# Self-attention and a frequency-split convolution: x loaded first in a turn, the scan and the low convolution later, the next image's scale and its value projection moved into the turn

## The chip, the cores and the metric

One core of one Trainium2 chip runs the whole program in one launch. The metric is device time in microseconds (us), lower is better. TensorE (PE) does the matmuls, ScalarE (ACT) exponentials and copies, VectorE (DVE) subtractions, maxima and sums, GpSimd (POOL) elementwise work and one reduction over partitions, SyncE (SP) issues all DMAs in one queue.

## The reference

x has 4 images of 256 channels and 64x64 pixels. Layer 0 is self-attention over the 4096 pixels of an image:

```
q = Wq x; k = Wk x; v = Wv x                    (32, 32 and 256 rows)
attn = softmax(q^T k / sqrt(32));  out = Wo (v attn^T);  x1 = gamma * out + x
```

Layer 1 works on each 8x8 patch of x1: `low` is the mean of 2x2 pixels, `high = p - up2(low)`; low goes through a 256x256 product, high and its copy rolled by one row go through a 256x512 product, each with a bias, a batch norm and a PReLU, and the output is `up2(low) + high`.

## The kernel before, in words

An image is cut into 8 chunks of 512 pixels, so there are 32 turns, one per chunk of queries. The values are not v but u = (Wo Wv) x, scaled by a number found from the largest |x| of the image so that they fit a pair of fp16 tensors (`uh`, `ul`). All probabilities are fp16 pairs too, so a product is three matmuls. While turn g weighs the values of its own image, it also projects one chunk of the next image (plan FULL, 24 turns); the turns of the last image have no projection (plan LAST, 7 turns), and the last turn is FINAL.

A turn has 32 steps t in a fixed order, `UNITS`. Sixteen steps are key tiles "d" (scores S by L593, two exponentials on ACT, L761 and L764, the low half on DVE, L1046, then twelve matmuls, L634 to L636), and sixteen are slots "k". A slot's probabilities come from the scores that the turn before saved (`saved`), take two exponentials (L772, L773) and a subtraction on DVE (L1051), go through a DMA transpose (L373) into `pt`, and are weighed by twelve matmuls (L647 to L649). A slot is subtracted three or four steps ahead of its use, so that the transpose has time. The order is d0 to d5, then k0, d6, k1, d7 and so on, and the last six steps are k10 to k15.

In between a plan gives each step small tasks of PE that use the PSUM banks M0 and M1 in turn. A task that takes a bank waits until the one before it on that bank was read:

- `kq` and `u 0`, `u 1`: the next image's keys and queries, and its values in two halves (L485). ACT reads a value half with the image's scale (L784), DVE makes the low half (L1078).
- `max j m`: 32 score blocks of the next turn's queries, whose maxima DVE takes (L946, and L950 with saving). `DOUBLE` lists the steps that hold two.
- `negmax`: the maxima of the 512 queries transposed (L528), for the next turn's `qcur`, which `finish_q` builds on DVE (L964 and L965). The first scores of the next turn wait for it.
- `y 0`, `y 1`: the attention output transposed, plus x (L1058). `low` and `high`: the two products of layer 1 on it (L485), read by ACT (L791, L797).

The scale of the image after next's values comes from a scan: in turn c of an image DVE takes the maximum |x| of chunk c (L903) at step `SCAN`, from `xr`, after which the same buffer is loaded with the residual. At the start of an image `before_image` runs `find_scale`: DVE reduces the 8 maxima (L908), POOL reduces over partitions (L1188, L1189), DVE finishes in four small steps (L910 to L918). ACT waits for the result before the first turn of the image. This happens three times inside the loop (ahead of turns 0, 8 and 16) and once in the start.

SP's queue is in program order and holds, per turn, 16 transposes, the q, u, x and out transfers, and in the last turn of an image the reload of all u tiles. `turn_slot(g, k)` is one transpose with its waits; what stands between two `turn_slot` calls is issued between two transposes.

Of the kernel before, what the change touches and what calls it, by code (L numbers as in the profile page):

```python
# [26 lines left out]
B, C, HW = 4, 256, 64 * 64  # L27
# [6 lines left out]
ALL = B * NCH  # L34
# [10 lines left out]
ROUND_X, ROUND_CONV, SCAN, NEGATIVE = 9, 14, 12, 26  # L45

DOUBLE = (8, 10, 15, 17, 25)
# [38 lines left out]
def steps_with_maxima(steps, first=3, doubled=DOUBLE):  # L86

    left = list(MAXIMA)
    t = first
    while left:  # L90
        for _ in range(2 if t in doubled else 1):
            j, m = left.pop(0)
            assert m not in TURNED or t > LOW_AT[slot_of(j, m)]
            steps.setdefault(t, []).append(("max", j, m))
        t += 1
    steps[t] = [("negmax",)]
    return steps
# [3 lines left out]
FULL = Plan(steps_with_maxima({0: [("kq",), ("u", 0)], 2: [("u", 1)], 5: [("y", 0)], 6: [("y", 1)], 19: [("low", 0)],  # L101
                               20: [("low", 1)], 21: [("high", 0)], 23: [("high", 1)]}))

LAST = Plan(steps_with_maxima({4: [("y", 0)], 5: [("y", 1)], 19: [("low", 0, 1)], 21: [("high", 0)], 23: [("high", 1)]},
                              doubled=(8, 10, 12, 15, 17, 26)),
# [9 lines left out]
def attention_conv(nc, x, wqk, wv, wo, phase_w, mag_w, params, gamma, alpha, out, q_dram):  # L115
# [7 lines left out]
    with ctx:  # L123
# [133 lines left out]
        def turns(eng, turn, before_image=None, before_last=None, image_end=None):  # L257


            inner = NCH - 1 if image_end else NCH  # L260
            with eng.Fori(0, B // 2 - 1) as pair_i:
                for parity in range(2):
                    if before_image:
                        before_image(pair_i * 2 + parity, parity)
                    with eng.Fori(0, inner) as c:
                        turn(pair_i * (2 * NCH) + parity * NCH + c, parity, c, FULL, scans=True)
                    if image_end:
                        image_end(pair_i * (2 * NCH) + parity * NCH + inner, parity, inner, scans=True)

            if before_image:  # L270
                before_image(B - 2, 0)
            with eng.Fori(0, inner) as c:
                turn((B - 2) * NCH + c, 0, c, FULL, scans=False)
            if image_end:
                image_end((B - 2) * NCH + inner, 0, inner, scans=False)
            if before_last:
                before_last()
            with eng.Fori(0, NCH - 1) as c:
                turn((B - 1) * NCH + c, 1, c, LAST, scans=False)
            turn(ALL - 1, 1, NCH - 1, FINAL, scans=False)  # L280
# [46 lines left out]
        def _(sp):  # L327
# [63 lines left out]
            def turn(g, parity, c, plan, scans, ends_image=False):  # L391
                slot = c if isinstance(c, int) else ds(c, 1)
                flat = (lambda dram: dram[slot]) if isinstance(c, int) else (lambda dram: dram[slot].rearrange("k q n -> (k q) n"))
                if plan is FULL:

                    sp.wait_ge(qsave_ready, NCH + g + 1)
                    sp.dma_start(flat(q_dram), qsave[96:128, :]).then_inc(qsave_free, 16)
# [8 lines left out]
                if plan is FULL:  # L406
                    emptied(sp, plan, g, ("u", 1))
                    sp.dma_start(flat(uh_dram), uh_next_flat[:, :]).then_inc(u_stored, 16)
                    sp.dma_start(flat(ul_dram), ul_next_flat[:, :]).then_inc(u_stored, 16)
# [4 lines left out]
                if plan is FULL:  # L414

                    sp.wait_ge(x_split[0], EVEN_FIRST + g)
                    gk = (g + 1 + NCH) % ALL
                    sp.dma_start(xb[:, :, :], x_v[ds(gk // NCH, 1), ds(gk % NCH, 1)]).then_inc(xb_loaded, 16)
                if ends_image:
                    sp.wait_ge(u_stored, 32 * g + 64)  # L420
                    sp.sem_inc(turn_seen, 1)
                    load_direct_u(g, 0)
# [8 lines left out]
                turn_slot(g, 4)  # L431
                if ends_image:
                    load_direct_u(g, 1)
                turn_slot(g, 5)
                turn_slot(g, 6)
# [3 lines left out]
                if scans:  # L439
                    sp.wait_ge(xs_scanned, g + 2)  # L440
                    sp.dma_start(xr[:, :, :], x_v[ds(g // NCH, 1), ds(g % NCH, 1)]).then_inc(xr_loaded, 16)
# [7 lines left out]
                turn_slot(g, 11)  # L449
                turn_slot(g, 12)  # L450
# [5 lines left out]
                if ends_image:  # L456
                    load_turned_u(g, TURNED[2])
                    load_turned_u(g, TURNED[3])
# [239 lines left out]
        def _(act):  # L698
# [76 lines left out]
            def take(bank, task, g, parity, c):  # L775

                kind = task[0]
                if kind == "kq":
                    nc.scalar.activation(kst[0:96, ds(c * CH + (1 - parity) * HW, CH)], bank[0:96, :], ACT.Copy).then_inc(k_hi, 1)
                    act.wait_ge(qsave_free, 16 * (NCH + g + 1))  # L780
                    nc.scalar.activation(qsave[96:128, :], bank[96:128, :], ACT.Copy).then_inc(qsave_ready, 1)
                elif kind == "u":
                    act.wait_ge(u_stored, 32 * g + 32)
                    nc.scalar.activation(uh_next[:, 2 * task[1]:2 * task[1] + 2, 0:C],  # L784
                                         bank[:, :].rearrange("p (m n) -> p m n", n=C),
                                         ACT.Copy, scale=uscale[1 - parity][:, 0:1]).then_inc(u_hi, 1)
# [57 lines left out]
            def before_image(image, parity):  # L844
                act.wait_ge(scaled, image + 2)

            turns(act, turn, before_image)
# [13 lines left out]
        def _(dve):  # L861
# [43 lines left out]

            def find_scale(image, parity):

                nc.vector.tensor_reduce(bnd[:, 0:1], amax[:, parity, :], AX.X, ALU.max).then_inc(bound, 1)  # L908
# [15 lines left out]
            dve.wait_ge(scanned0, NCH)  # L924
            find_scale(0, 0)
# [34 lines left out]

            def finish_q(bank, count, free):

                dve.wait_ge(nhi_ready, count)
                nc.vector.tensor_copy(qcur[0:96, :], qst[0:96, :].bitcast(f32))  # L964
# [58 lines left out]
            nc.vector.tensor_copy(nhi[96:128, :], M[n % 2][96:128, :]).then_inc(nhi_ready, 1)  # L1023
            finish_q(M[n % 2], 1, m_free[n % 2])
# [7 lines left out]
            def normalise(g):  # L1032
# [4 lines left out]
                gain = ogain[:, B - 1:B] if isinstance(g, int) else ogain[:, ds((g + (ALL - 1)) % ALL // NCH, 1)]  # L1037
# [59 lines left out]
            def finish_chunk(g):  # L1097

                dve.wait_ge(s_filled, ND * g + ND)
                finish_q(M[1], g + 2, m_free[1])  # L1100

            def turn(g, parity, c, plan, scans):
# [6 lines left out]
                for t in range(MT):  # L1109
# [6 lines left out]
                    if t == 1 and plan is not FINAL:  # L1116
                        low_q(g + 2)
                    if t == SCAN and scans:
# [7 lines left out]
                    if t == NEGATIVE:  # L1126
                        negative_parts(plan, g)
                if plan is FULL:
                    finish_chunk(g)

            def before_image(image, parity):

                dve.wait_ge(xs_scanned, image * NCH + 1)
                find_scale(image + 1, 1 - parity)

            turns(dve, turn, before_image)
# [127 lines left out]
```

## Time and profile before

| | us |
|---|---|
| median of 3 runs (lowest, highest) | 2344.87 (2343.41, 2346.97) |
| the profiled execution | 2340.0 |
| its span | 2337.9 |
| PE busy in the span | 2211.3 (95%) |
| DVE busy | 1753.7 (75%) |
| ACT busy | 1436.5 (61%) |
| POOL busy | 679.7 (29%) |
| mean granted clock of TensorE, as a share of full | 0.985 |

The span is the profiled execution without what lies around it (2.1 us). A busy PE in this view is not PE at its peak, since matmuls are drawn with their whole pipeline and overlap one another. What tells more is from which instruction to which the time runs, and what ended an idle stretch.

### The profile page before, as it was taken

The numbers are of one execution on the slowest core, as the hardware profiler recorded it, in microseconds if no ns is written. First come the engines' busy times: TensorE is split into PE (matmuls) and PEld (weight loads), VectorE is DVE, ScalarE is ACT, GpSimd is POOL, SyncE is SP. The second block draws the span as 40 slices with busy tenths as digits, with TensorE's granted clock in tenths as the row PEclk, the third lists the DMA queues.
The fourth block names the chain that finished last, engine by engine and source line by source line (L and its number), as shares of the span: only waits on it lengthen the run. The fifth ranks groups of instructions, "written<-read, shape, count | busy, mean of one in ns | idle before, by whom it ended". The sixth has DMA issues, their size and how long they took to land.

```text
span 2337.9 us, 48151 instructions
## 1 busy us (share of the span) xinstructions
PE 2211.3 (95%) x16373; PEld 1763.5 (75%) x16373; DVE 1753.7 (75%) x3388; ACT 1436.5 (61%) x2547; POOL 679.7 (29%) x891
## 2 busy tenths in 40 slices
PE   5799999999989999999998999999999999999997
PEld 4577777777767777777776877777777777777776
DVE  6777787777767777877776777777877777778764
ACT  3456666656656666666665666576666656666664
POOL 3232332232322323322332222323322232233221
PEclk8799999999999999999999999999999999999998
DMA  5154444355553554443474433544445444344443
GB/s 167 44 113 112 99 103 109 71 112 113 133 131 72 109 116 99 105 105 81 100 169 103 101 83 75 111 98 95 103 106 131 83 93 88 76 84 89 84 86 67
DMA packets 596617, 235.02 MB, mean 101 GB/s; under 512 B 547072, under 2 KB 548352, under 8 KB 596576
## 3 DMA queue, kind: packets, MB, share of 16 engines
q1 hardware_dynamic: 596576, 234.51, 45.7%
q8 instruction: 22, 0.36, 0.1%
q14 instruction: 19, 0.16, 0.0%
HBM read 67.67 MB, written 32.53 MB: 43 GB/s over the span
## 4 chain that ended last, share of the span: by engine, by line
PE 69%; DVE 11%; issue 8%; DMA 5%; ACT 4%; SPq 1%; POOL 1%; DVEq 0%; ACTq 0%; POOLq 0%
PE M L485 13%; PE M L522 8%; PE O L647 7%; PE O L634 7%; PE O L649 7%; PE O L636 7%; PE O L648 7%; PE O L635 7%; PE S L593 4%; DVE pq L1051 3%; DMA xr<-in_x 2%; DVE pmax L946 2%; DMA pt<-pq 2%; DVE saved L950 2%; DVE pl L1046 1%
## 5 line engine op out<-in xcount | busy, mean ns | idle before, releaser
L761 ACT ACTIVATE ph<-S 128x512 f16<-128x512 f32 x512 | 307.1, 600 | 480.5 <-PE S L593 479.4
L647 PE MATMUL O<-uh,pt 128*128 128x257 f16 x2048 | 568.5, 278 | 9.6 <-DMA pt<-pq 9.1
L950 DVE TENSOR_SCALAR_CACHE_REDUCE saved<-M 128x512 f32<-128x512 f32 x512 | 346.1, 687 | 305.8 <-PE M L522 303.5
L634 PE MATMUL O<-uh,ph 128*128 128x257 f16 x2048 | 570.4, 278 | 4.2 <-DVE pl L1046 3.8
L636 PE MATMUL O<-uh,pl 128*128 128x257 f16 x2048 | 563.2, 275 | 0.0
L635 PE MATMUL O<-ul,ph 128*128 128x256 f16 x2048 | 561.9, 274 | 0.0
L649 PE MATMUL O<-uh,pt 128*128 128x257 f16 x2048 | 558.9, 273 | 0.0
L648 PE MATMUL O<-ul,pt 128*128 128x256 f16 x2048 | 555.7, 271 | 0.0
L522 PE MATMUL M<-kst,qst 96*128 (+1 forms) x1024 | 435.7, 447 | 25.6 <-DVE pmax L946 13.3
L1046 DVE TENSOR_TENSOR pl<-p,ph 128x512 f16<-128x512 f32 x512 | 396.4, 775 | 53.8 <-ACT p L764 52.4
L772 ACT ACTIVATE pq<-saved,nbias 128x512 f16<-128x512 f32 x512 | 369.2, 721 | 47.3 <-DMA pt<-pq 47.3
L1051 DVE TENSOR_TENSOR pq<-saved,pq 128x512 f16<-128x512 f32 x512 | 383.8, 750 | 19.2 <-ACT saved L773 19.0
L946 DVE TENSOR_REDUCE pmax<-M 128x1 f32<-128x512 f32 (+1 forms) x512 | 339.9, 683 | 40.1 <-PE M L522 38.1
L773 ACT ACTIVATE saved<-saved,nbias 128x512 f32<-128x512 f32 x512 | 367.7, 718 | 0.0
L764 ACT ACTIVATE p<-S 128x512 f32<-128x512 f32 x512 | 307.6, 601 | 0.0
L634 PEld LDWEIGHTS O<-uh,ph 128*128 128x128 f16 x2048 | 201.0, 98 | 131.2 <-issue 90.5
L647 PEld LDWEIGHTS O<-uh,pt 128*128 128x128 f16 x2048 | 198.8, 97 | 110.3 <-issue 37.6
L593 PE MATMUL S<-qcur,kst 128*128 128x512 f32 x512 | 238.2, 475 | 18.5 <-ACT p L764 16.1
L1212 POOL TENSOR_TENSOR zlow<-zlow,zlneg 128x256 f32<-128x256 f32 x32 | 23.6, 737 | 786.2 <-DVE zneg L1066 786.2
L522 PEld LDWEIGHTS M<-kst,qst 96*128 96x128 f32 x1024 | 187.1, 191 | 76.2 <-DVE pmax L946 33.0
L636 PEld LDWEIGHTS O<-uh,pl 128*128 128x128 f16 x2048 | 201.7, 99 | 26.2
L649 PEld LDWEIGHTS O<-uh,pt 128*128 128x128 f16 x2048 | 197.7, 97 | 29.2
(161 smaller groups left out, 2887.7 us busy)
## 6 DMA issues: line engine op xcount, KB each, us to landing
xr<-in_x SPq DMA_DIRECT2D x53, 512.0 KB, 3.7
out_y<-z SPq DMA_DIRECT2D x33, 512.0 KB, 3.0
xb<-in_x SPq DMA_DIRECT2D x25, 512.0 KB, 3.8
pt<-pq SPq DMA_TRANSPOSE x512, 3.1
qraw<-q_scratch SPq DMA_DIRECT2D x99, 64.0 KB, 1.9
uh_scratch<-uh_next SPq DMA_DIRECT2D x24, 257.0 KB, 3.0
uh<-uh_scratch SPq DMA_DIRECT2D x24, 257.0 KB, 3.2
ul_scratch<-ul_next SPq DMA_DIRECT2D x24, 256.0 KB, 2.9
```

Source lines behind the costliest of these rows:

```text
L522: return nc.tensor.matmul(bank[:, :], qst[0:96, j * 128:(j + 1) * 128], kst[0:96, keys_at], start=True, stop=True)
L634: nc.tensor.matmul(O[j][:, 0:UW], ph[:, i % 4, q], uh[:, i, :], start=(i == 0), stop=False)
L635: nc.tensor.matmul(O[j][:, 0:C], ph[:, i % 4, q], ul[:, i, :], start=False, stop=False)
L636: ins = nc.tensor.matmul(O[j][:, 0:UW], pl[:, i % 4, q], uh[:, i, :], start=False, stop=False)
L647: nc.tensor.matmul(O[j][:, 0:UW], pt[:, k % RING, i, :], uh[:, t, :], start=False, stop=False)
L648: nc.tensor.matmul(O[j][:, 0:C], pt[:, k % RING, i, :], ul[:, t, :], start=False, stop=False)
L649: ins = nc.tensor.matmul(O[j][:, 0:UW], pt[:, k % RING, SUB + i, :], uh[:, t, :], start=False, stop=(ends and i == SUB - 1))
L772: nc.scalar.activation(pq[:, k % RING, 0, :], saved[:, k, :], ACT.Exp, scale=SCALE, bias=bias)
L946: nc.vector.tensor_reduce(pmax[:, j, ds(m, 1)], bank[:, :], AX.X, ALU.max).then_inc(free, 1)
L950: nc.vector.tensor_scalar(saved[:, slot_of(j, m), :], bank[:, :], 0.0, None, ALU.add, ALU.max, accum_out=pmax[:, j, m:m + 1]).then_inc(fre ...
L1046: nc.vector.tensor_tensor(pl[:, i % 4, :], p32[:, i % 2, :], ph[:, i % 4, :], ALU.subtract).then_inc(lo_ready, 1)
L1051: nc.vector.tensor_tensor(pq[:, k % RING, 1, :], saved[:, k, :], pq[:, k % RING, 0, :], ALU.subtract).then_inc(slot_low, 1)
```

## The change

Eight edits in one:

1. SP issues the load of the next chunk to project (`xb`) first in a turn. Before, it stood behind slot 2.
2. The rounding of that chunk on ACT goes from step 9 to 10, the scan from step 12 to 20, and the residual's load from behind slot 7 to behind slot 11.
3. In FULL, `u 0` goes from step 0 to 7 and `u 1` from step 2 to 8. SP stores the result behind slot 5 (before: behind slot 1).
4. `low`, `high 0`, `high 1` go from steps 19 (and 20), 21, 23 to 20 (and 21), 22, 24.
5. The steps with two maxima are 11, 13, 15, 16, 18, 25 (before: 8, 10, 15, 17, 25, and for LAST 8, 10, 12, 15, 17, 26). In FULL the last maximum is at step 28 rather than 29, `negmax` stays at 30, so that a slot lies between them. In LAST both stay at 28 and 29.
6. The copy of 96 rows of `qcur` (L964) leaves the end of the turn for step 27 (`start_q`). The wait for the turn's last scores goes with it.
7. At the start of an image DVE only reduces the 8 maxima (`bound_x`). The rest of `find_scale` is done at step 4 of the image's first turn, and ACT waits for it at `u 0`.
8. In the last turn of an image SP reloads the u chunks 0 and 1 and the first turned one behind slot 6 (before: behind slots 2, 4 and 6), and waits for the u store at the end of the turn.

```diff
-ROUND_X, ROUND_CONV, SCAN, NEGATIVE = 9, 14, 12, 26
+ROUND_X, ROUND_CONV, SCAN, NEGATIVE, QUERIES, RESCALE = 10, 14, 20, 26, 27, 4
-DOUBLE = (8, 10, 15, 17, 25)
+DOUBLE = (11, 13, 15, 16, 18, 25)
-    steps[t] = [("negmax",)]
+    steps[t - 1 + negmax_after] = [("negmax",)]
-FULL = Plan(steps_with_maxima({0: [("kq",), ("u", 0)], 2: [("u", 1)], 5: [("y", 0)], 6: [("y", 1)], 19: [("low", 0)],
-                               20: [("low", 1)], 21: [("high", 0)], 23: [("high", 1)]}))
+FULL = Plan(steps_with_maxima({0: [("kq",)], 7: [("u", 0)], 8: [("u", 1)], 5: [("y", 0)], 6: [("y", 1)], 20: [("low", 0)],
+                               21: [("low", 1)], 22: [("high", 0)], 24: [("high", 1)]}, negmax_after=2))
...
@@ SP's turn
                 if plan is FULL:
+                    sp.wait_ge(x_split[0], EVEN_FIRST + g)
+                    gk = (g + 1 + NCH) % ALL
+                    sp.dma_start(xb[:, :, :], x_v[ds(gk // NCH, 1), ds(gk % NCH, 1)]).then_inc(xb_loaded, 16)
                     sp.wait_ge(qsave_ready, NCH + g + 1)
...
                 turn_slot(g, 5)
+                if plan is FULL:
+                    emptied(sp, plan, g, ("u", 1))
+                    sp.dma_start(flat(uh_dram), uh_next_flat[:, :]).then_inc(u_stored, 16)
+                    sp.dma_start(flat(ul_dram), ul_next_flat[:, :]).then_inc(u_stored, 16)
                 turn_slot(g, 6)
                 if ends_image:
+                    load_direct_u(g, 0)
                     load_direct_u(g, 1)
                     load_turned_u(g, TURNED[0])
...
@@ ACT, taking u
-                    act.wait_ge(u_stored, 32 * g + 32)
+                    if task[1] == 0:
+                        act.wait_ge(scaled, g // NCH + 2)
+                        act.wait_ge(u_stored, 32 * g + 32)
...
@@ DVE
+            def bound_x(parity):
+                nc.vector.tensor_reduce(bnd[:, 0:1], amax[:, parity, :], AX.X, ALU.max).then_inc(bound, 1)
...
+            def start_q():
+                nc.vector.tensor_copy(qcur[0:96, :], qst[0:96, :].bitcast(f32))
...
+                    if t == RESCALE and scale_of is not None:
+                        find_scale(scale_of + 1, 1 - parity)
...
+                    if t == QUERIES and plan is not FINAL:
+                        dve.wait_ge(s_filled, ND * g + ND)
+                        start_q()
...
             def before_image(image, parity):
                 dve.wait_ge(xs_scanned, image * NCH + 1)
-                find_scale(image + 1, 1 - parity)
+                bound_x(1 - parity)
```

## Rows read from the trace of the kernel before

**Rows 1.** The page's busy times of the engines over the span.
```profile
PE 2211.3 (95%) x16373; PEld 1763.5 (75%) x16373; DVE 1753.7 (75%) x3388; ACT 1436.5 (61%) x2547; POOL 679.7 (29%) x891
```

**Rows 2.** Who waited for whom: engine, line <- releaser: us in total, times, longest.
```profile
ACT oraw L755 <- DVE uscale L918: 55.0, 3, 21.4
...
DVE prod L910 <- POOL bndall L1189: 27.5, 4, 7.3
...
PE M L528 <- DVE nmax L957: 17.0, 32, 1.3
...
PE M L522 <- DVE pmax L946: 13.3, 19, 1.3
...
PE M L485 <- ACT zlow L791: 12.1, 24, 0.5
```

**Rows 3.** The chain of waits: start us, us, what.
```profile
247.56 1.40 PE M L485 x12
...
597.32 1.40 PE M L485 x12
...
677.37 1.41 PE M L485 x12
...
748.25 1.40 PE M L485 x12
...
1247.17 1.40 PE M L485 x12
...
1317.24 1.40 PE M L485 x12
...
1386.22 1.40 PE M L485 x12
```

**Rows 4.** Timeline ahead of turn 8: start us, us, what [idle <-releaser].
```profile
661.17 0.16 DVE L908 TENSOR_REDUCE bnd<-amax 128x1 f32<-128x8 f32 x1
...
668.34 0.16 DVE L910 TENSOR_TENSOR prod<-bndall 128x1 f32<-128x1 f32 x1 [7.01 <-POOL bndall L1189]
...
670.84 0.80 PE L593 MATMUL S<-qcur,kst 128*128 128x512 f32 x1 [5.95 <-ACT p L764]
```

**Rows 5.** Busy times of one stretch, and the granted clock (0.74).
```profile
665.00:675.00 10.00, 4.04 (x16) 2.46 (x17) 4.76 (x16) 5.52 (x12) 0.38 (x1) 0.74 0.04 8
```

**Rows 6.** Timeline at an ordinary turn's start (turn 4): PE, ACT, DVE.
```profile
380.06 0.72 PE L593 MATMUL S<-qcur,kst 128*128 128x512 f32 x2
...
382.02 0.63 PE L485 MATMUL M<-wu,xbh 128*128 128x256 f32 x4
...
383.66 0.28 PE L634 MATMUL O<-uh,ph 128*128 128x257 f16 x1
...
384.90 0.48 PE L593 MATMUL S<-qcur,kst 128*128 128x512 f32 x1
...
386.08 0.75 DVE L1078 SCALAR_TENSOR_TENSOR ul_next<-M,uscale,uh_next 128x512 f16<-128x512 f32 x1
...
386.74 0.68 DVE L1046 TENSOR_TENSOR pl<-p,ph 128x512 f16<-128x512 f32 x1
```

**Rows 7.** Timeline at the scan and at negmax (turn 3), and in turn 7.
```profile
339.60 1.22 DVE L903 TENSOR_REDUCE amax<-xr 128x1024 f32 x1 [1.13 <-DMA xr<-in_x]
...
341.48 0.50 PE L522 MATMUL M<-kst,qst 96*128 x1 [0.70 <-DVE pmax L946]
...
377.04 0.62 PE L528 MATMUL M<-ident,nmax 128*128 128x128 f32 x4 [0.38 <-DVE nmax L957]
...
618.69 0.28 PE L647 MATMUL O<-uh,pt 128*128 128x257 f16 x1 [1.10 <-DMA pt<-pq]
```

**Rows 8.** Timeline of ACT at step 7 of turn 3.
```profile
328.29 0.60 ACT L761 ACTIVATE ph<-S 128x512 f16<-128x512 f32 x1 [2.10 <-PE S L593]
...
329.87 0.72 ACT L773 ACTIVATE saved<-saved,nbias 128x512 f32<-128x512 f32 x1
```

**Rows 9.** Line L964 on DVE: shortest, median and longest ns.
```profile
L964 DVE CAST qcur<-qst x32: 424/664/768, 89.7 to 2251.9; 96x512 fp32r<-96x512 f32 x32
```

## What the change was predicted to do, and why

> **What bounds the kernel now.** I read four views. The page's busy times come first: TensorE is busy for 2211.3 of 2337.9 us [rows 1]. Its own arithmetic stays the same in this change (the same tasks in another order), so only the time in which it stands can be won. The wait list names the ends of those stands: `negmax` on DVE's maxima (17.0 us, 32 times), score blocks on DVE's `pmax` (13.3 us, 19 times), the low product on ACT's `zlow` (12.1 us, 24 times, never over 0.5), and, the largest single ones, ACT on the image's scale (three times, up to 21.4 us), behind which DVE waits for POOL's reduction (four times, up to 7.3 us) [rows 2]. The chain of waits gives the length of a turn, from one turn's second value block (`u 1`) to the next one's: (597.32 - 247.56) / 5 = 69.95 us for a turn with a scan, 1386.22 - 1317.24 = 68.98 us for one without. But from 597.32 to 677.37, over the start of an image, it is 80.05 us, and the turn behind that is 70.88 us, not 69.9 [rows 3]. The timeline shows the reason: DVE reduces the maxima at 661.17, gets POOL's answer at 668.34, and TensorE scores again at 670.84 [rows 4]. In the ten microseconds from 665 the granted clock is 0.74 on average, that is partly the lower of the two levels [rows 5], and the work before it is back at 2.4 GHz ends about at 677.
>
> A stall is somewhat more than the idle time in a row: a weighing matmul is drawn 0.27 to 0.28 us long and the next one may start some 0.03 us behind the last one's start, so I add 0.24 us to each idle figure.
>
> **The change part by part.** All terms are against the profiled execution (2340.0 us, span 2337.9, 2.1 around it). The median of the runs is 2344.87, 0.2% above it; I take differences and subtract them from the median.
>
> *Boundary of images (edit 7), ahead of turns 0, 8 and 16.* The stand between bound and score goes: POOL's 7.2 us (668.34 - 661.17) now runs beside turn work, since DVE asks for the result only at step 4. That step is about 11 us into a turn (step 3's score blocks follow `u 1`, which stands at 677.37 less the boundary's excess, 6.7 us behind the turn's first score), so the answer is there with 4 us to spare. For turn 8 the excess is 80.05 - 69.95 = 10.1, of which I leave 0.8 to the last turn of an image (below): -9.3. Turn 16 the same: 1247.17 - 748.25 = 498.92 for seven turns, 10 more than seven of 69.8: -9.3. Turn 0 follows the start-up, where PE has gaps and a low clock anyway, and about 3 us of the low clock stay (half speed over some 6 us): -6. Sum **-24.6**. The five small DVE operations and their waits, 0.85 to 1.0 us, now stand between step 4's work and `max 0 1`; PE waits behind it for the bank for 0 to 0.9, I take 0.4, times 3: **+1.2**. The turn behind a boundary was 1.0 us too long three times (70.88 against 69.9; 70.07 against 68.98) [rows 3]. Its cause I can't see; between 0 and -3.2 I take **-1.5**.
>
> *`u 0` out of step 0 and `u 1` out of step 2 (edit 3, all 24 FULL turns).* These 24 matmuls, 2.8 us, were cover. At a turn's start PE has two scores (380.06), `kq`, then `u 0` from 382.02, one score and the first tile at 383.66 [rows 6]. Without `u 0` it is ready for that tile at about 382.25, while DVE's `pl` of tile 0 is there at about 382.4: 0.15 of stall. Then score and tile (1.24 from 383.66 to 384.90, so some 1.56 for both), again both, and at 385.6 PE wants tile 2. DVE is at that time in `normalise` and `kst`, and begins `pl` of tile 2 at 386.08, where the old `ul_next` stood (386.08, and `pl` behind it at 386.74): tile 2 starts at 386.8, stall 1.2. Together +1.35. Not less than 0.9, since DVE's order is given; not more than 2.8, since then all cover would be lost. At step 7 ACT first makes two exponentials of the tile and two of slot 3, from 328.29 to 330.5, 0.5 us behind the score [rows 8], and only then reads `u 0` (0.6), DVE follows with 0.7: bank M1 is free 4.1 us behind the score's start, while PE arrives at `u 1` 3.2 us behind it (score 0.32, `u 0` 1.40, a maximum 0.24, a tile 1.25): +0.9, between 0.3 and 1.6. Sum per turn **+2.25**, the price of the whole change, 54 us over 24 turns.
>
> *What pays for it.* (a) The low product at steps 20 and 21: the slot k7 now lies between its two halves and ACT has no exponentials of a slot in step 20, so the wait of 0.5 + 0.24 goes: -0.7 [rows 2]. (b) `negmax` one slot behind the last maximum. The wait is 0.38 + 0.24 in turn 3 [rows 7]. One slot is 1.25 us more room, the moved copy of `qcur` takes 0.66 of it on DVE [rows 9]: -0.5. (c) The scan. At step 12 DVE waits 1.13 us for `xr` and then scans for 1.22, and PE stalls 0.70 + 0.24 one step later [rows 7]. At step 20 the load is long there and DVE has idle time behind it, since the high product holds PE for 2.8 us. A scan turn is longer than one without by 69.95 - 68.98 = 0.97, which is the most that this can give; I take -0.85, in 16 turns. (d) Doubled maxima at other steps: DVE is not behind from step 7 to 12 any more. The other waits for `pmax` and `saved` come to between 0 and 1.1 us a turn; I take -0.7.
>
> So a turn without a scan: 2.25 - 0.7 - 0.5 - 0.7 = +0.35, times 8: **+2.8**. With a scan: -0.5, times 16: **-8.0**.
>
> *Where a moved copy meets GpSimd.* The copy of `qcur` moves from the end of the turn to step 27, just when POOL adds up the output. In the trace it takes 424 ns at the start, where POOL stands, and 664 in the median [rows 9].
> The Trainium skill (SBUF — State Buffer, the section on who interferes with whom) says that a VectorE copy in a two-port mode and a GpSimd instruction exclude each other for their whole length. Row 9 agrees in its two levels. By that rule the copy could wait for a whole GpSimd addition, at most 0.8 us, and the sum would be some 15 us higher if the copy always did and nothing hid it.
> My sum takes 0.66 from the row, with 0.42 and 0.77 as bounds.
>
> *SP's queue (edits 1, 2, 8).* `xb` first in a turn stands behind slot 15's transpose, which therefore is not delayed; it clears the busiest place, behind slot 2. The u stores come behind slot 5, the residual behind slot 11. For a plain turn 0, between -0.3 and +0.6. In an image's last turn before, PE waited 1.10 us for a transpose [rows 7]; that goes, about -0.8 with what follows, times 3. But now six loads, 1.5 MB, stand between slots 6 and 7, and slot 7's transpose is late by 1 to 2.4 us: +1.5, times 3. Sum **+1.7**, from -2 to +6.
>
> *LAST (7 turns).* There is no value work. Its maxima move too (-0.9, for the same reason as in (d)), while `negmax` gets no room and the copy of `qcur` stands before the last maximum: +0.45. **-3**, between -7 and +5.
>
> Sum: -24.6 + 1.2 - 1.5 + 2.8 - 8.0 + 1.7 - 3 = -31.4. Forecast 2344.9 - 32 = **2313 us**; in a profiled execution some 2308.
>
> **The rivals.**
>
> 1. *Only the boundaries pay, less a little; the turn gets longer.* What is won at low, negmax and scan in a turn (1.9 without (c), 2.75 with it) comes out smaller than the 2.25 lost. If a turn is longer by 0.5 us on average, it is -25 + 12 - 3 = -16: 2329. For it: DVE's total is unchanged, so what is moved from one stretch comes back in another.
> 2. *The turn gains more.* DVE catches up between steps 9 and 20 and (d) is worth 1.1, the start costs 0.9. Then a turn gains about 1.1 and it is -25 - 26 + 3 = 2297. For it: after `u 1` DVE has less per step than PE in each pair of steps.
> 3. *Slower.* One mechanism: the uncovered start. If PE stalls for tile 0, 1 and 2 for the whole 2.8 us that `u 0` and `u 1` covered, and for the whole 1.6 at `u 1`, a turn loses 4.4 and wins 2.4 on average, +2.0 x 24 = 48 against the boundaries' 25: +20, 2365. It decides from a net loss of 1.1 us a turn on (25 / 24). Against it: DVE's order at the start leaves no later time than 386.8 for tile 2.
> 4. *The reduction isn't hidden.* POOL's 7.2 us were measured with DVE standing; beside a busy DVE it may take longer. From 11 us on DVE waits in step 4 and all stand again: the boundary gives 5 less each, 2328.
>
> **How the numbers follow.** Forecast 0.52, rival 1 0.17, rival 2 0.17, rival 3 0.06, rival 4 0.08. The range that leaves out no more than 2 in 10 goes from rival 2's near side to rival 1: **2294 to 2330**. 0.2% is 4.7 us, about what a measurement of this kernel can tell from no change. Faster by more than that 0.92, within it 0.03, slower 0.05.
>
> **What would show it.** Right: the four `u 1`-to-`u 1` excesses of 10 us are gone and the clock stays at 1.0 from turn 1 on; ACT's wait for `uscale` is gone from the list; a new PE wait of about 1 us per turn, 24 times, for DVE `pl` at tile 2, and another for `ul_next` at `u 1`; none for `zlow`; no wait of DVE for `xr`; equal turns, about 69.4 us, with and without a scan. Wrong: a wait for POOL's `bndall` in step 4, PE waits for `pt` at k4 to k7, or a plain turn of 70.5 us or more.

## The result: 1.4% slower, and the profile after

The changed kernel takes 2376.47 us (median of 4 runs, 2376.24 to 2376.82), the kernel before beside it 2344.19 (4 runs). The ratio is 1.0139, with a 95% interval from 1.0127 to 1.0151. Timed again on another chip (`changed_again`) it is 1.0159 (1.0145 to 1.0173). The forecast was 2313, a gain of 1.4%: wrong in sign, by 63 us. The profiled execution has a span of 2374.8 us against 2337.9.

Below, a percentage is a ratio to the kernel before on the same chip; 0.1% is 2.3 us. Chips differ (the kernel before took 2336.5 to 2344.2), so two variants are compared by their ratios.

The page after, busy times of the engines:

```profile
PE 2208.2 (93%) x16373; PEld 1759.7 (74%) x16373; DVE 1769.3 (75%) x3388; ACT 1433.2 (60%) x2547; POOL 655.8 (28%) x891
```

TensorE is busy as long as before [rows 1] in a span 37 us longer: it stands more. The wait list after (engine, line <- releaser: us, times, longest):

```profile
DVE ul_next L1085 <- ACT uh_next L786: 77.0, 48, 3.4
...
PE O L634 <- DVE pl L1053: 29.3, 61, 0.9
...
PE M L528 <- DVE nmax L960: 21.5, 32, 1.7
...
PE M L485 <- DVE ul_next L1085: 19.0, 24, 0.8
...
PE M L522 <- DVE pmax L949: 17.2, 31, 0.7
...
PE M L485 <- ACT zlow L793: 11.3, 23, 0.5
...
DVE prod L912 <- POOL bndall L1201: 6.5, 1, 6.5
```

Against [rows 2]: the one wait for POOL's `bndall` that is left is the start's (6.5 us, once, before 27.5, four times), and the waits of ACT for `uscale` ahead of an image are out of the list. So edit 7 does what it says. But `zlow` is still there (11.3, 23 times, before 12.1, 24 times), `nmax` has grown from 17.0 to 21.5 (in the last image's turns, 0.96 to 1.67 each; in a FULL turn it goes from 0.38 to 0.35), `pmax` from 13.3 to 17.2, and two new ones stand beside them: PE for `pl` (29.3) and PE for `ul_next` (19.0, 24 times). Both had been forecast. The first row is what stands behind the latter: VectorE waits 77.0 us in all for ScalarE's half.

The chain of waits gives the length of a turn, at the second value block as in [rows 3]:

```profile
330.29 1.68 PE M L485 x12
...
402.16 1.68 PE M L485 x12
...
617.69 1.68 PE M L485 x12
...
695.28 1.68 PE M L485 x12
...
1345.41 1.68 PE M L485 x12
...
1417.22 1.68 PE M L485 x12
```

402.16 - 330.29 = 71.87 us for a turn with a scan (before 69.95), 1417.22 - 1345.41 = 71.81 without (before 68.98), and 695.28 - 617.69 = 77.59 over the end of one image and the start of the next (before 80.05). So the two kinds of turn are equal now, as forecast, but at 71.8 and not 69.4. PE's longest stands in one turn (and, last, in turn 7), from the timeline:

```profile
388.79 0.28 PE L634 MATMUL O<-uh,ph 128*128 128x257 f16 x1 [0.91 <-DVE pl L1053]
...
402.16 0.50 PE L485 MATMUL M<-wu,xbh 128*128 128x256 f32 x2 [0.78 <-DVE ul_next L1085]
...
413.47 0.50 PE L522 MATMUL M<-kst,qst 96*128 x1 [0.56 <-DVE pmax L949]
...
421.40 0.50 PE L522 MATMUL M<-kst,qst 96*128 x1 [0.46 <-DVE saved L953]
...
432.08 0.50 PE L485 MATMUL M<-hh,wp 128*128 128x512 f32 x1 [0.50 <-ACT zlow L793]
...
450.86 0.62 PE L528 MATMUL M<-ident,nmax 128*128 128x128 f32 x4 [0.35 <-DVE nmax L960]
...
645.84 0.40 PE L647 MATMUL O<-uh,pt 128*128 128x257 f16 x1 [2.57 <-DMA pt<-pq]
```

Each is one idle time with its releaser: 0.91 at tile 2 for `pl`, 0.78 at the second value block, 0.56 at step 13 and 0.46 at step 17 for a maximum, 0.50 at the high product for `zlow`, 0.35 at `negmax`; in the last turn of an image 2.57 for slot 7's transpose. VectorE in the same turn:

```profile
401.36 0.75 DVE L1085 SCALAR_TENSOR_TENSOR ul_next<-M,uscale,uh_next 128x512 f16<-128x512 f32 x1 [2.90 <-ACT uh_next L786]
...
410.54 1.14 DVE L1058 TENSOR_TENSOR pq<-saved,pq 128x512 f16<-128x512 f32 x1
...
411.60 1.21 DVE L1053 TENSOR_TENSOR pl<-p,ph 128x512 f16<-128x512 f32 x1
...
448.47 0.94 DVE L966 CAST qcur<-qst 96x512 fp32r<-96x512 f32 x1
```

Waiting for ScalarE it stands 2.90 us; later the two subtractions with two inputs that begin at 410.54 and 411.60 last 1.14 and 1.21 us as drawn (0.68 in most other places), and the moved copy 0.94 instead of the 0.66 that I took [rows 9].

### The profile page after: what moved, and what is told of

Read it like the earlier page. It is cut to its first block, busy times and chain, and to the rows that moved or that the text cites. A ratio compares the mean times of both kernels' runs of the same rounds, so it can differ in the third digit from the quotient of the medians.

```text
span 2374.8 us, 47957 instructions
## 1 busy us (share of the span) xinstructions
PE 2208.2 (93%) x16373; PEld 1759.7 (74%) x16373; DVE 1769.3 (75%) x3388; ACT 1433.2 (60%) x2547; POOL 655.8 (28%) x891
## 4 chain that ended last, share of the span: by engine, by line
PE 59%; DVE 19%; issue 10%; ACT 8%; DMA 2%; SPq 1%; DVEq 1%; ACTq 0%; POOL 0%; POOLq 0%
PE M L485 11%; PE M L522 7%; PE O L647 6%; PE O L649 6%; PE O L648 6%; PE O L634 6%; PE O L636 5%; PE O L635 5%; DVE pq L1058 4%; DVE saved L953 4%; PE S L593 3%; DVE pl L1053 3%; DVE pmax L949 3%; ACT p L764 2%; DMA pt<-pq 2%
## 5 line engine op out<-in xcount | busy, mean ns | idle before, releaser
L634 PE MATMUL O<-uh,ph 128*128 128x257 f16 x2048 | 567.8, 277 | 29.3 <-DVE pl L1053 29.3
L522 PE MATMUL M<-kst,qst 96*128 (+1 forms) x1024 | 423.4, 441 | 32.3 <-DVE pmax L949 17.2
L1053 DVE TENSOR_TENSOR pl<-p,ph 128x512 f16<-128x512 f32 x512 | 382.2, 748 | 78.1 <-ACT p L764 76.0
L1058 DVE TENSOR_TENSOR pq<-saved,pq 128x512 f16<-128x512 f32 x512 | 390.9, 763 | 19.7 <-ACT saved L773 19.6
```

The lines of the kernel that those rows point to most:

```text
L522: return nc.tensor.matmul(bank[:, :], qst[0:96, j * 128:(j + 1) * 128], kst[0:96, keys_at], start=True, stop=True)
L634: nc.tensor.matmul(O[j][:, 0:UW], ph[:, i % 4, q], uh[:, i, :], start=(i == 0), stop=False)
L1053: nc.vector.tensor_tensor(pl[:, i % 4, :], p32[:, i % 2, :], ph[:, i % 4, :], ALU.subtract).then_inc(lo_ready, 1)
L1058: nc.vector.tensor_tensor(pq[:, k % RING, 1, :], saved[:, k, :], pq[:, k % RING, 0, :], ALU.subtract).then_inc(slot_low, 1)
```

## The experiments

The changed kernel itself was run again beside two of the variants:

> The changed kernel itself, beside the next two on one chip, as the reference for the differences of single edits that were taken from ratios on other chips. Expected ratio to the kernel before 1.012 to 1.015.

1.0159, a little above the first ratio. Where not said otherwise, a kernel is the changed one with one thing altered; a `...` in a diff stands for lines left out. The ratio of the changed kernel stands at 1.014 to 1.016.

| kernel | ratio to before | interval |
|---|---|---|
| undo_value_and_scale | 1.0000 | 0.9991 to 1.0010 |
| undo_scale_only | 1.0229 | 1.0212 to 1.0247 |
| value_and_scale_alone (on before) | 1.0232 | 1.0218 to 1.0246 |
| act_reads_low_first | 1.0085 | 1.0068 to 1.0102 |
| undo_query_copy | 1.0075 | 1.0058 to 1.0092 |
| less_gpsimd | 1.0056 | 1.0039 to 1.0073 |
| act_reads_u_first | 1.0085 | 1.0068 to 1.0102 |
| undo_reload_order | 1.0102 | 1.0085 to 1.0119 |
| undo_x_load | 1.0119 | 1.0102 to 1.0136 |
| mended | 0.9881 | 0.9864 to 0.9897 |
| early_scale (on before) | 0.9906 | 0.9890 to 0.9923 |
| early_scale_2 (on before) | 0.9898 | 0.9883 to 0.9914 |
| combined | 0.9727 | 0.9711 to 0.9743 |
| combined_old_doubles | 0.9712 | 0.9696 to 0.9729 |

**The value projection and the scale.**

```diff
-FULL = Plan(steps_with_maxima({0: [("kq",)], 7: [("u", 0)], 8: [("u", 1)],
+FULL = Plan(steps_with_maxima({0: [("kq",), ("u", 0)], 2: [("u", 1)],
...
                 bound_x(1 - parity)
+                find_scale(image + 1, 1 - parity)
```

> The changed kernel with the value projection back at steps 0 and 2, and with it the whole scale computation back before the image (it is needed there); everything else as changed. Theory (the projection at steps 7 and 8 costs more in each turn than I priced: TensorE stalls of 1.4 us at the start and 1.1 us at the second value block, and then 1.8 us more in steps 11 to 17 because VectorE stood 2.9 us behind ScalarE and is late): these 4.3 us go in 24 turns, the two boundaries cost their 10 us again and the start 8: a turn of 68.0 to 68.5 us, 2376 - 85 + 25 = about 2316. Rival A (the late maxima and SP's order make the turn long, the projection is only a part): a turn of 70 us or more and about 2355. Rival B (the moved low product, scan and query copy are worth nothing): as the kernel before, 2344.

It is as fast as the kernel before, to 0.1%; rival B was right. In its trace an ordinary turn is 69.3 to 69.4 us with or without a scan. So edits 1, 2, 4, 5, 6 and 8 together are worth nothing where the projection isn't moved: a scan turn is 0.5 shorter, one without 0.4 longer. And the projection costs 71.85 - 69.4 = 2.45 us a turn in the changed kernel. In my expectation I had laid the stalls of steps 11 to 17 to it too, and that was half right: PE's idle time at steps 13 and 17 is 0.56 and 0.46 us in the changed kernel and 0.29 and 0.29 here.

```profile
405.65 0.50 PE L522 MATMUL M<-kst,qst 96*128 x1 [0.29 <-DVE pmax L951]
...
413.43 0.50 PE L522 MATMUL M<-kst,qst 96*128 x1 [0.29 <-DVE saved L955]
```

In the kernel before, the turns without a scan have 0.33 us of such idle time at the maxima on average (four of the eight only 0.12 or 0.13); here every turn has about 0.6.

Only the scale back, the projection left at 7 and 8 (the same diff without its change of FULL):

> The changed kernel, but the whole scale is again found before an image's first turn; the value projection stays at steps 7 and 8. It measures the gain of edit 7 by itself. Theory: the 7 us between bound and score come back three times, with the low clock behind them, +8 to +9 each: +25 us, 2395 to 2400. Rival (part of that stand is covered by work that the changed kernel has waiting there, or the low clock was most of it): +15.

Its ratio lies 0.7 to 0.9% above the changed kernel's, 16 to 21 us, and its span 20 us above (2395.2 against 2374.8): between theory and rival. PE's wait at the first scores is back (its wait list, three times and the start):

```profile
PE S L593 <- ACT p L764: 20.5, 4, 7.2
```

The other way round, only edits 3 and 7 on the kernel before:

```diff
+FULL = Plan(steps_with_maxima({0: [("kq",)], 7: [("u", 0)], 8: [("u", 1)], 5: [("y", 0)], 6: [("y", 1)], 19: [("low", 0)],
...
+                    if t == RESCALE and scale_of is not None:
+                        find_scale(scale_of + 1, 1 - parity)
```

> The kernel before with only the value projection at steps 7 and 8 and the scale taken up at step 4 (SP's store of u behind slot 5, its wait before the last reload); x load, scan, residual, low and high products, maxima, query copy and reload order stand as before. Theory A (the price of the moved projection is made by its own two places, 1.4 us at tile 2 and 1.1 us at the second half, whatever stands around it): 2.45 us a turn, 59 us, less 21 for the scale: +38, 2377. Theory B (in the old surroundings it costs more, because two maxima in step 8 and two in step 10 stand right behind the second half and VectorE is late by 2.9 us): 3.5 us a turn, +60, 2400. Rival C (the old surroundings cover it better: TensorE waits for VectorE there anyway): 1.5 us a turn, +15, 2355.

+2.3% is +54 us, nearest to theory B. Its turns are 73.2 us with a scan and 72.6 without, so the projection costs 3.3 and 3.6 us a turn in the old surroundings. The wait list of that kernel (L488 is the second value block, L525 a maximum):

```profile
PE M L525 <- DVE ul_next L1088: 31.9, 24, 1.3
...
PE M L488 <- DVE ul_next L1088: 18.9, 24, 0.8
```

The second row is the wait that the changed kernel has too; the first, 31.9 us in 24 turns, stands at step 8, where two maxima follow and one of them wants the bank of the second half. The changed kernel, with its doubles from step 11 on, doesn't have it. So the moved maxima, which gain nothing by themselves, save about 1 us a turn of the projection's price. The wait lists point to them; they were not moved alone under a projection at 7 and 8.

**The four places that were to pay.** The low product:

```diff
+                    early = any(task[0] == "low" for n, task in plan.numbered.get(t, []))
                     for k in range(NK):
-                        if EXP_AT[k] == t:
+                        if EXP_AT[k] == t and not early:
                             slot_probabilities(g, k)
...
+                        if EXP_AT[k] == t and early:
```

> The changed kernel, but at step 21 ScalarE reads the second low product before it makes slot 10's two exponentials. Theory: the low product's stall did not go with the move, it went from the second low block to the high block behind it, because the same bank is asked for one tile after a block that ScalarE reads behind two exponentials (0.75 us in every FULL turn, before and after). Read first, it goes: -0.75 x 24 = -18 us, a turn of 71.1. Rival (ScalarE's exponentials of slot 10 then come late for VectorE and the transpose): no gain, or a new wait at k10.

The wait for `zlow` is out of the list, and an ordinary turn is 70.7 to 71.1. In time it is 0.5 to 0.7%, 13 to 17 us; the forecast 18 was a little high.

The query copy:

```diff
             def finish_chunk(g):

+                dve.wait_ge(s_filled, ND * g + ND)
+                start_q()
...
                     if t == QUERIES and plan is not FINAL:
-                        dve.wait_ge(s_filled, ND * g + ND)
-                        start_q()
+                        pass
```

> The changed kernel with only the copy of qcur's 96 rows back at the end of the turn. Theory: at step 27 the copy takes 0.9 us beside GpSimd's additions and stands before the last maximum, so it makes the 0.67 us stall at negmax in FULL and adds 0.7 in LAST; without it negmax does not wait in FULL. At the turn's end it may cost at most 0.1. Expected -0.6 x 24 - 0.6 x 7 = -18 us: 2358. Rival: VectorE is late there anyway because of the doubled maximum of step 25; then the stall stays and the time is 2376 or a little more.

15 to 20 us. `negmax` waits no more in the FULL turns; the eight times left are those of the last image and the start:

```profile
PE M L528 <- DVE nmax L960: 7.0, 8, 1.3
```

A FULL turn is 70.9 to 71.3, one of the last image 64.9 against 65.7 in the changed kernel and 65.5 before. So the slot between the last maximum and `negmax` did open the room that I had counted on, and the moved copy took all of it. The rival is out: with step 25 still doubled the wait goes.

GpSimd beside the doubled maxima:

```diff
-                    low_x(0, xbl, xb, xbh, g + EVEN_FIRST + 1)
+                    pool.wait_ge(x_hi[0], g + EVEN_FIRST + 1)
+                    nc.gpsimd.tensor_tensor(xbl[:, 0, 0:8], xb[:, 0, 0:8], xbh[:, 0, 0:8].bitcast(f32),
+                                            ALU.subtract).then_inc(x_split[0], 1)
```

> The changed kernel, with the low halves of the next chunk of x left out but for 8 columns, so that GpSimd has 3.2 us less in steps 11 and 12 of each FULL turn (the projected keys and values are less exact by that). Theory: VectorE's subtractions at steps 11 and 12 last 1.1 us instead of 0.6 because GpSimd works at the same time, and with two maxima in step 11 and again in 13 that makes the stall of 0.83 us at step 13; it goes, the one at step 17 (0.61, beside the convolution's low halves) stays: -0.8 x 24 = -19 us. Rival (the banks and the doubled maxima alone make it): no change.

20 to 24 us; 19 had been expected. This kernel leaves the low halves of x out but for 8 columns, so it is a measurement and no repair. The two operations at steps 11 and 12 are short again, and PE's wait for `pmax` is down from 17.2 us in 31 to 4.3 in 7:

```profile
1402.83 0.68 DVE L1058 TENSOR_TENSOR pq<-saved,pq 128x512 f16<-128x512 f32 x1
...
1403.43 0.68 DVE L1053 TENSOR_TENSOR pl<-p,ph 128x512 f16<-128x512 f32 x1
```

```profile
PE M L522 <- DVE pmax L949: 4.3, 7, 1.0
```

That shows the cause of the step 13 stall: with two maxima there and two in step 11 VectorE has no time to spare, and beside GpSimd's 3.2 us it comes late. The stall of step 17, which I had expected to stay, goes too: PE's idle time at the maxima falls from 1.02 us to 0.17 in an ordinary turn, and the turn from 71.8 to 70.7.

The doubled maxima by themselves, in the best kernel:

```diff
-DOUBLE = (11, 13, 15, 16, 18, 25)
+DOUBLE = (8, 10, 15, 17, 19, 25)
```

> The kernel combined (68.0 us a turn) with the doubled maxima at steps 8, 10, 15, 17, 19, 25 rather than 11, 13, 15, 16, 18, 25. It measures edit 5's places. Theory: steps 11 and 13 are where GpSimd takes the next chunk's low halves and VectorE's two-input operations are slowed, so doubles there cost 0.6 us at step 13; at 8 and 10 GpSimd works on the frequency split and slows VectorE as well: within 0.3 us a turn of combined, 2272 +- 7. Rival (the earlier doubles use VectorE's idle time better): 67.4 us a turn, 2258.

0.15% apart, inside the intervals: with the projection at 0 and 2 the choice between these two sets of doubles decides nothing. (The old set of FULL had five, without 19.)

**ScalarE's order at step 7**, the same swap for `u 0`:

```diff
+                    early = plan is FULL and t == 7
```

> The changed kernel, but at step 7 ScalarE reads the first value half before it makes slot 3's two exponentials. Theory: the bank is free 1.2 us earlier, so the 1.1 us stall at the second value half goes, VectorE waits 1.7 instead of 2.9 us and part of the 1.8 us of stalls in steps 11 to 17 goes: -1.1 to -2.5 us a turn, 2320 to 2350. Rival (the stalls of steps 11 to 17 come from doubled maxima meeting GpSimd's work, which has VectorE's two-input instructions last 1.1 us instead of 0.7): only the 1.1 goes, and the slot's exponentials 0.7 later cost nothing: 2350.

13 to 17 us; PE's wait for `ul_next` at the second half is out of the list. The stalls of steps 13 and 17 stay as they were (0.57 and 0.46), so the rival described it better than the theory.

**The reload order.**

```diff
+                if ends_image:
+                    load_direct_u(g, 0)
                 turn_slot(g, 3)
...
+                if ends_image:
+                    load_direct_u(g, 1)
                 turn_slot(g, 5)
...
                 turn_slot(g, 6)
-                if ends_image:
-                    load_direct_u(g, 0)
-                    load_direct_u(g, 1)
```

> The changed kernel with the reload of the u chunks 0 and 1 back behind slots 2 and 4 in an image's last turn (the wait for the u store stays at the end). Theory: slot 7's transpose stood behind six loads, which is the 2.8 us stall at k7 and most of the 4.7, 3.4 and 2.0 us by which the last turns of the images exceed 71.8 us; they become 72 to 73: -6 to -9 us, 2368. Rival (the last turn is long because of the u store's place behind slot 5, or of the x load that now follows the reload): no change, 2376.

9 to 13 us. PE's waits for a transpose fall from 8.8 us (longest 2.6) to the row below, and the last turn of an image is 71.5 to 71.9 us, as long as any other:

```profile
PE O L648 <- DMA pt<-pq: 2.8, 6, 0.9
```

**The x load** back behind slot 2:

```diff
                 turn_slot(g, 2)
+                if plan is FULL:
+                    sp.wait_ge(x_split[0], EVEN_FIRST + g)
+                    gk = (g + 1 + NCH) % ALL
+                    sp.dma_start(xb[:, :, :], x_v[ds(gk // NCH, 1), ds(gk % NCH, 1)]).then_inc(xb_loaded, 16)
```

> The changed kernel with the load of the next chunk back behind slot 2. It measures edit 1. Theory: nothing waits for that load in either kernel longer than 1.5 us, and no transpose is late for it: within 4 us of the changed kernel, 2371. Rival (the early load delays slot 15's transpose or the q store at the turn's start): 5 to 10 us less.

1.0119 against 1.0139 and 1.0159: 5 to 9 us less, though its interval meets that of the first ratio. Edit 1 gains nothing, and the trace says that it costs a little, by a way that neither theory nor rival named. With the load back behind slot 2, ScalarE waits for it (29.3 us in 24 turns, in the changed kernel never), GpSimd's low halves begin 31.5 and 31.3 us behind `negmax` in turns 4 and 18 and not 30.0, and PE's idle time at the maxima of an ordinary turn is about 0.6 us and not 1.02; the waits for a transpose stay (9.1 us against 8.8). The early load had put GpSimd's work right beside the doubled maxima.

**Four repairs at once, projection still at 7 and 8** (the diffs of act_reads_low_first, act_reads_u_first, undo_query_copy and undo_reload_order):

> The changed kernel with four small repairs and the value projection still at steps 7 and 8: ScalarE reads the first value half and the low product before the slot's exponentials, the query copy is back at the turn's end, the reload order is back. Alone these gave about -11, -12, -15 and -7.5 us. Theory: each removes a wait at a place of its own, so they add up: -45, 2326 where the changed kernel has 2371, that is 10 us below the kernel before. Rival (they overlap: a TensorE that arrives earlier waits for VectorE at the doubled maxima): -25 to -35, about equal to the kernel before.

0.9881: 28 us below the kernel before and 60 to 65 below the changed one, more than the 45 expected. The 45 came from single ratios that I compared with one reading of the changed kernel. In the profiled spans the four are 16.7, 17.1, 22.1 and 12.3 below 2374.8, together 68, and mended is 2310.0, 65 below: they add up. A FULL turn is 69.5 to 69.8. Its wait list has the projection's price at tile 2 left (and the maxima of steps 13 and 17, in all 17.7 us for `pmax` and 13.0 for `saved`), and nothing of FULL at `negmax`:

```profile
PE O L635 <- DVE pl L1058: 29.2, 60, 0.9
...
PE M L529 <- DVE nmax L965: 7.0, 8, 1.3
```

**The scale early, on the kernel before.** `early_scale` and `early_scale_2` differ in one factor of one turn: in the first, the last turn of the third image is normalised with another image's factor. The instructions are the same.

```diff
+            bound_x(1)
...
                         scan(amax[:, parity, ds(c, 1)], xr[:, :, :], xs_scanned)
+                        if ends_image:
+                            dve.wait_ge(xs_scanned, g + 2)
+                            bound_x(parity)
+                    if t == 23 and scans and ends_image:
+                        find_scale(g // NCH + 2, parity)
...
                 low_conv_in(pool, nc.gpsimd, g)
+                if ends_image and scans:
+                    reduce_bound(g // NCH + 2)
```

> The kernel before, with nothing moved but the scale: the maxima are reduced right behind the last scan of an image (step 13 of its last turn), GpSimd reduces over partitions behind the convolution's low halves, VectorE finishes at step 23; for the first image of the loop it is begun behind the start's last scan. The value projection stays at steps 0 and 2. Theory: the 10 us ahead of turns 8 and 16 go and 6 to 8 of turn 0, no ordinary turn changes: -27 to -30 us against the kernel before, 2310. Rival (the clock or the first turn's stalls come back elsewhere, or GpSimd's reduction beside a busy VectorE takes so long that it delays the output): -10 to -20.

> early_scale with the third image's last turn reading its own image's factor in the normalisation (in early_scale that one turn took another image's); no instruction is added or taken away. Expected the time of early_scale: 21 to 25 us below the kernel before, an exact copy of its turns.

0.9906 (0.9890 to 0.9923) and 0.9898: 22 and 24 us. That is nearly the whole stand ahead of the images, without moving the projection: from one `negmax` to the next, the first turns of the second and third image take 70.2 and 70.5 us in the trace of early_scale_2 (before: 80.1 and 79.7), that of the first 73.6 (before: 80.1). POOL's reduction in the last turn of the first image (timeline of early_scale_2):

```profile
621.30 0.19 POOL L1194 TENSOR_TENSOR bndspare<-bnd 128x1 f32<-128x1 f32 x1
...
627.80 0.38 POOL L1195 PARTITION_ALL_REDUCE bndall<-bnd  x1 [6.32 <-issue]
```

6.50 us from the first row to the second, beside a VectorE that works for most of that time; in the kernel before, with VectorE standing, it is 6.52 (661.41 to 667.93).

**Combined**: projection at steps 0 and 2, scale early, query copy at the turn's end, old reload order, low product read first.

> The changed kernel with the value projection back at steps 0 and 2, the scale taken early as in early_scale, the query copy back at the turn's end, the reload order back, and the low product read first. Theory: 69.35 us a turn (measured with projection and scale back) less 0.67 at negmax and 0.75 at the high block, so 67.9 to 68.0 us, no boundary: 24 x 1.4 + 27 + 5 for the last image = 65 us below the kernel before, about 2275. Rival (the gains overlap: TensorE then waits for VectorE at the doubled maxima): 68.5 us a turn, 2290.

0.9727: 64 us or 2.7% below the kernel before, the fastest of all with its variant. A FULL turn but the first is 67.8 to 68.1 us, over an image boundary 68.7, one of the last image 64.9. Three second value blocks from its chain of waits, 68.05 and 68.01 us apart, and what is left of PE's waits for VectorE:

```profile
442.64 1.40 PE M L486 x12
...
510.69 1.40 PE M L486 x12
...
578.70 1.40 PE M L486 x12
```

```profile
PE M L523 <- DVE saved L960: 11.9, 31, 1.9
...
PE M L523 <- DVE pmax L956: 9.6, 27, 0.7
...
PE M L529 <- DVE nmax L967: 7.0, 8, 1.3
```

## Why the prediction was wrong, point by point

*What bounds the kernel, and the arithmetic.* Right: PE's busy time is 2208.2 against 2211.3, all of the difference is stands. One sum is off by 0.4 us: SP's terms, three times -0.8 and three times +1.5, give +2.1 and not +1.7.

*The boundary (-24.6 + 1.2).* Mechanism right, size high by a few us: 16 to 21 measured by undo_scale_only. The granted clock is 1.00 from 671 to 681 us, over the start of the second image, DVE never waits for POOL in step 4, and rival 4 (the reduction not hidden) did not happen. PE's stand behind step 4's small operations is 0.49 and 0.51 us ahead of a maximum in turns 8 and 16 (taken: 0.4). The 1.0 us by which the turn behind a boundary was too long, whose cause I could not see, is gone too; in turn 8 of the kernel before two waits for a transpose stand there, 0.76 and 0.72 us, and the changed kernel has none.

*The projection (+2.25 a turn).* Right, with a little luck in the number. By its rows: 0.91 + 0.24 at tile 2 and 0.78 + 0.24 at the second half, the two places that I named, and 0.22 at tile 0; by the experiment 2.45. But some 0.4 of the 2.45 lie at steps 13 and 17, where I had put nothing. What I had not seen is that in the old surroundings it would have cost 3.3 to 3.6.

*What pays for it.* This is the step that failed. I took -1.9 without and -2.75 with a scan; measured, with the projection undone, +0.4 and -0.5. Over 24 turns that is 54 of the 63 us. Term by term:

(a) Low product, -0.7, got 0. I had placed only the bank between its two halves. The high product asks for the same bank one tile behind the second half, and ScalarE has slot 10's exponentials in step 21 just as it had slot 9's in step 19: the 0.50 us went from the low row to the high row of the same list (12.1 us, 24 times, to 11.3, 23 times). Shown by act_reads_low_first.

(b) `negmax`, -0.5, got 0. Room of one slot, 1.25 us, less the copy. I priced the copy by its median, 0.66, and left out that VectorE stands at the last maximum later by that and by what is doubled in step 25. The copy took 0.94 (median of its 32 executions), and the last maximum starts right behind it, at 449.34. Shown by undo_query_copy.
The Trainium skill (SBUF — State Buffer, who interferes with whom) has a VectorE copy in a two-port mode and a GpSimd instruction exclude each other for a whole instruction. The trace agrees with it: 0.94 us beside GpSimd's additions of 0.7 to 0.9 us, against 0.42 alone. Undoing the copy gave 15 to 20 us, but that takes away the whole copy from its place; that it is this exclusion which lengthens it was not isolated.

(c) The scan, -0.85 in 16 turns. Right: turns with and without a scan are equal, within 0.4 us, in every kernel that scans at step 20.

(d) Doubled maxima elsewhere, -0.7, got +0.4, and here is the sign: they cost. The before list's waits for `pmax` were counted as if new places had none. With the projection back (undo_value_and_scale) PE stands about 0.6 us at steps 13 and 17 of every turn, where a turn without a scan had 0.33 on average before. Steps 11 to 13 have GpSimd's low halves beside them, which with the early load begin 1.3 to 1.5 us sooner than with the load behind slot 2; without them (less_gpsimd) 0.17 is left. The 0.4 is what is left of the turn's change when (a) and (b) are nothing; edit 5 was not run alone on the kernel before.

*SP's queue (+1.7).* The mechanism (slot 7 behind six loads) was right, the size was not: 9 to 13 us. I counted one stall of 1 to 2.4 us, +1.5 on average; the three are 2.57, 1.73 and 2.08 idle, and in two of them the clock fell (below). For the x load I took 0; undo_x_load puts its cost at 5 to 9 us more.

*LAST (-3).* Got +2 (65.5 to 65.7 a turn). Without the copy a turn is 64.9, so the rest of the change does gain 0.6 of the 0.9 that I took (PE's idle time at step 17's maximum goes from 0.42 to 0.17, that for `zlow` from 0.18 to nothing), but the copy costs 0.8 where I took 0.45: the wait at `negmax` is 1.67 with it and 0.81 without.

*Rival 3* had the sign, and put its break-even at a net loss of 1.1 us a turn. The loss was 1.9 to 2.8, but by its other half: the start did not cost more than forecast, the payers paid nothing.

## What to carry to other kernels

A stall that goes with a bank or an in-order engine is not gone when the task is moved: before counting it as a gain, look up who next asks for that bank and what the reading engine has in front of it at the new step. Price each new place as if it had the waits of its neighbours, not none, and look at what the third engine does at that time. And when a wait ahead of a phase is the target, first ask whether its cause can be started earlier (early_scale: -23 us alone) before moving the work that needs the result later, since that work may be what covers the start of each turn.

## What the runs showed of the hardware that I had not expected

- A stand of 2.57 us of PE ahead of k7 in turn 7, behind dense matmuls, is followed by the lower clock. The granted clock from 645 to 650 us is 0.50 (1.2 GHz), a weighing matmul is drawn 0.40 us long (645.84 above) and twelve of them take 2.41 us in the timeline instead of 1.25; with what follows, this stand of 2.6 us cost about 5 (turn 7 is 76.6 us from `negmax` to `negmax`, with the reload order back 71.5):

```profile
645.00:650.00 5.00, 4.16 (x20) 3.36 (x20) 0.00 (x0) 0.94 (x2) 0.00 (x0) 0.50 0.56 158
```

  It is not so each time: ahead of the same slot in turn 15 PE stands 1.73 us and the granted clock is 0.50 from 1226 to 1228 us, in turn 23 it stands 2.08 us and the clock is 1.00 from 1801 to 1809. These turns are 3.3 and 2.0 us too long.

- The reduction over partitions on GpSimd takes 6.5 us whether VectorE works beside it or not (6.50 in early_scale_2, 6.52 before), nearly all of it ahead of the 0.38 us that are drawn as its work.
- VectorE's two-input subtractions last 1.14 and 1.21 us beside GpSimd's work and 0.68 without it (less_gpsimd). GpSimd's are drawn longer at times too: 1.18 us instead of 0.73 for the last of the four low halves of x in turns 4 and 18 of the changed kernel.
